# Regrouping VectorE's activation steps in the feed-forward phase of a pre-norm transformer layer: one group per tile instead of three lockstep stages over three tiles

## The reference

```python
x = x + attn(_layernorm(x), w_qkv, b_qkv, w_proj, b_proj)
# feed-forward, on _layernorm(x), w1: 1024 x 4096, w2: 4096 x 1024
h = float2fix(x @ w1 + b1, 8)             # round to multiples of 1/256
y = interp(h, 33 points of exact GELU on [-4, 4])
y = where(h > 4, h, where(h < -4, 0, y))
h = float2fix(y, 8)
out = float2fix(h @ w2 + b2, 8)
x = x + out
```

## Time and profile before

| what | us |
|---|---|
| median of 2 runs | 4179.5 (4175.3 and 4183.7) |
| the profiled execution | 4143.4 |
| its span on the slowest core (core 3), first to last instruction | 4141.9 |
| spans of the 8 cores | 4116.6 to 4141.9 |
| TensorE busy | 2703.5 (65%) |
| ScalarE busy | 2370.2 (57%) |
| VectorE busy | 2022.8 (49%) |
| GpSimd busy | 667.4 (16%) |

### The profile page before, as it was taken

One profiled execution on the slowest core, in us unless ns is written; L12 is line 12 of the kernel. 1 busy time (PEld: TensorE's weight loads), 2 busy tenths in 40 slices (PEclk: granted clock), 3 DMA queues, 4 the chain that ended last, 5 costly groups with the idle time before them and its releaser, 6 DMA issues.

```text
span 4141.9 us, 39884 instructions; the slowest of 8 cores (4116.6 to 4141.9 us)
## 1 busy us (share of the span) xinstructions
PE 2703.5 (65%) x10880; PEld 940.8 (23%) x10880; DVE 2022.8 (49%) x3166; ACT 2370.2 (57%) x2861; POOL 667.4 (16%) x1234
## 2 busy tenths in 40 slices
PE   0594757676769876768683455656665666667676
PEld 0241212111114311111111112222222222222222
DVE  2114434343430343434343466666767576666774
ACT  1223848484833484848481466666656566666662
POOL 1010000000001000000002233232323232332330
PEclk9997989898989998989896557877787777877788
DMA  5122010101022001010104533343434343443441
GB/s 105 51 31 92 29 54 28 48 4 43 4 63 33 10 4 43 4 43 4 43 4 102 92 56 55 63 64 63 68 67 71 54 79 52 68 65 65 59 77 44
DMA packets 204565, 207.43 MB, mean 50 GB/s; under 512 B 23744, under 2 KB 167104, under 8 KB 204352
## 3 DMA queue, kind: packets, MB, share of 16 engines
q0 software_dynamic: 169792, 95.82, 18.4%
q1 hardware_dynamic: 34560, 109.07, 8.0%
HBM read 257.52 MB, written 33.55 MB: 70 GB/s over the span
## 4 chain that ended last, share of the span: by engine, by line
PE 29%; DVE 18%; ACT 15%; DVEq 12%; ACTq 11%; issue 7%; DMA 7%; POOL 1%; SPq 0%; POOLq 0%
ACT PTb L625 12%; PE pAT L639 6%; PE pA L329 5%; DVEq L1035 5%; ACTq L995 5%; DMA xstream<-x 5%; PE pA L612 5%; ACTq L975 4%; PE pBT L641 3%; DVE ft L1016 3%; PE pA L1079 3%; PE pA L363 3%; DVEq L1018 3%; DVE ft L1025 2%; DVE fki L1010 2%
## 5 line engine op out<-in xcount | busy, mean ns | idle before, releaser
L625 ACT ACTIVATE PTb<-pA,negB 128x1024 bf16<-128x1024 f32 x1024 | 1106.3, 1113 | 473.8 <-PE pA L615 451.5
L937 PE MATMUL pA<-xn,w1s 128*128 128x512 bf16 x2048 | 672.1, 491 | 548.6 <-ACT ft L951 528.7
L798 POOL DMA_DIRECT2D w1s<-w x1024 | 556.7, 577 | 1221.3 <-PE pA L937 1196.9
L639 PE MATMUL pAT<-PTb,vtm 128*65 128x512 bf16 x1024 | 409.3, 400 | 271.0 <-ACT PTb L625 201.9
L1079 PE MATMUL pA<-w2b,gbuf 128*128 128x512 bf16 x2048 | 483.5, 397 | 77.4 <-DVEq L1018 45.0
L937 PEld LDWEIGHTS pA<-xn,w1s 128*128 128x128 bf16 x2048 | 225.6, 116 | 960.9 <-issue 841.9
L612 PE MATMUL pA<-qfm,kfm 64*128 64x512 bf16 x1024 | 404.5, 405 | 51.9 <-DVEq L713 50.6
L641 PE MATMUL pBT<-PTb,vtm 128*65 128x512 bf16 x1024 | 408.4, 399 | 0.0
L615 PE MATMUL pA<-qfm,kfm 64*128 64x512 bf16 x1024 | 404.7, 405 | 0.0
L963 ACT ACTIVATE fu<-ft,p 128x512 f32<-128x512 f32 x256 | 183.9, 718 | 298.6 <-DVEq L1035 298.6
L1010 DVE TENSOR_SCALAR fki<-ft 128x512 f32<-128x512 f32 x256 | 109.7, 429 | 471.4 <-ACT fji L978 450.4
(11 more groups left out here) (90 smaller groups left out, 3103.9 us busy)
## 6 DMA issues: line engine op xcount, KB each, us to landing
w1s<-w POOLq DMA_DIRECT2D x1024, 64.0 KB, 2.6
xstream<-x SPq DMA_DIRECT2D x80, 512.0 KB, 3.8
x1rd<-x1s SPq DMA_DIRECT2D x64, 512.0 KB, 5.7
x1s<-x1t SPq DMA_DIRECT2D x32, 512.0 KB, 2.9
out<-outt SPq DMA_DIRECT2D x64, 256.0 KB, 2.7
wstr<-wqkv POOLq DMA_DIRECT2D x96, 128.0 KB, 5.8
w2b<-w POOLq DMA_DIRECT2D x32, 256.0 KB, 25.5
attn<-stgB POOLq DMA_DIRECT2D x64, 64.0 KB, 1.9
```

What stands on the lines that cost most here:

```text
L625: sc.activation(PT[:, kt % 2, :], pA[:, off:off + 1024], AF.Exp, bias=negB[:, 0:1], scale=SCALE).then_inc(c_s.sem, 1)
L639: t.matmul(pAT[0:65, :], lhs[:, 2 * pr, :], PT[:, kt % 2, 0:512], start=(kt == 0), stop=(kt == NKT - 1), skip_group_check=True)
L798: gp.dma_start(out=w1s[:, sl, dc, :], in_=w1[dc * 128:(dc + 1) * 128, grp * 256:(grp + 1) * 256]).then_inc(c_lw[sl].sem, 16)
L937: ins = t.matmul(pA[:, hb * 512:(hb + 1) * 512], w1s[:, sl, dc, (hm % 2) * 128:(hm % 2 + 1) * 128], xn2[:, bi % 2, dc, :], start=(dc == 0) ...
```

## The change

VectorE's eight instructions per tile are no longer arranged in the stages P, Q and R over three tiles. Each of ScalarE's steps gets VectorE's work on the same tile right behind it: `act_E012(g)` holds the w1 product, S1 and VectorE's first two instructions (called Va below), `act_E34(g-1)` holds S2 and the next three (Vb), `act_E56(g-2)` holds S3 and the last three (Vc), `act_E78(g-3)` holds S4. Within Va, Vb and Vc every instruction needs the one before it and a drain stands between them; the last one carries the signal itself, with no drain behind it. The order of ScalarE's instructions stays. Core of the diff:

```diff
-        def act_S1(h):
+        def act_E012(h):
...
-            def ev(sc, hm=hm, hb=hb, i4=i4, w=w1_pe, vg=incQ.get(h - 2)):
+            def ev(sc, hm=hm, hb=hb, i4=i4, w=w1_pe, vg=e6_hist.get(h - 4)):
...
+            def ev(v, i=i, i4=i4, w=sid_done, sg=e5_hist.get(h - 3)):
+                v.wait_ge(c_s.sem, w)
+                if sg is not None:
+                    v.wait_ge(c_s.sem, sg)
+                v.tensor_scalar(fki[:, i4, :], ft[:, i4, :], -1152.5, 1152.5,
+                                ALU.max, ALU.min)
+                v.drain()
+                v.tensor_scalar(ft[:, i4, :], fki[:, i4, :], MC, -MC,
+                                ALU.add, ALU.add).then_inc(c_v.sem, 1)
...
-            def ev(sc, i=i, i4=i4, w=incQ[h]):
+            def ev(sc, i=i, i4=i4, w=e1_hist[(h, "va")]):
...
+            def ev(v, i=i, i4=i4, w=u5_done):
+                v.wait_ge(c_s.sem, w)
+                v.tensor_scalar(fki[:, i4, :], fu5[:, i, :], MC, -MC, ALU.add, ALU.add)
+                v.drain()
+                v.scalar_tensor_tensor(ft[:, i4, :], fki[:, i4, :], -1.0, fu5[:, i, :],
+                                       ALU.mult, ALU.add)
+                v.drain()
+                v.tensor_scalar(fu5[:, i, :], ft[:, i4, :], 0.5, None,
+                                ALU.add).then_inc(c_v.sem, 1)
...
-            def ev(sc, i4=i4, j=j, w=incP[h + 1]):
+            def ev(sc, i=i, j=j, w=e1_hist[(h, "vb")], fg=e6_hist.get(h - 2)):
                 sc.wait_ge(c_v.sem, w)
+                if fg is not None:
+                    sc.wait_ge(c_v.sem, fg)
...
+            def ev(v, i=i, i4=i4, j=j, w=s3_done):
+                v.wait_ge(c_s.sem, w)
+                v.tensor_sub(ft[:, i4, :], fji[:, j, :], fgl[:, j, :])
+                v.drain()
...
+                v.drain()
+                v.scalar_tensor_tensor(fu5[:, i, :], fgl[:, j, :], 256.0, fki[:, i4, :],
+                                       ALU.mult, ALU.add).then_inc(c_v.sem, 1)
...
-            def ev(sc, bi=bi, hm=hm, i=i, j=j, w=incR[h + 2],
+            def ev(sc, bi=bi, hm=hm, i=i, j=j, w=e6_hist[h],
...
-        w2mm_marks = (4, 7, 10, 13, 16, 19, 22, 25)
-        w2ev_marks = (6, 9, 12, 15, 18, 21, 24, 27)
+        w2mm_marks = (3, 6, 9, 12, 15, 18, 21, 24)
+        w2ev_marks = (5, 8, 11, 14, 17, 20, 23, 26)
...
-                act_S1(g)
+                act_E012(g)
...
-            if 0 <= g - 1 < NG:
-                act_S2(g - 1)
-            if 0 <= g - 2 < NG:
-                act_S3(g - 2)
-            if 0 <= g - 3 < NG:
-                act_S4(g - 3)
+            if g >= 1 and g - 1 < NG:
+                act_E34(g - 1)
+            if g >= 2 and g - 2 < NG:
+                act_E56(g - 2)
+            if g >= 3 and g - 3 < NG:
+                act_E78(g - 3)
...
-            if g <= NG + 1:
-                act_V(g, NG)
```

More of the change, by code:

```diff
@@ L914, in build @@
         e5_hist = {}
+        e6_hist = {}
         e8_hist = {}
[L916 to L919, removed]
-        def act_S1(h):
+        def act_E012(h):
             bi, hm = divmod(h, 32)
             hb = hm % 2
+            i = h % 3
             i4 = h % 4
@@ L955, in act_S1, with act_E34 @@
             e1_hist[h] = c_s.n
-        def act_S2(h):
+            sid_done = c_s.n
+            def ev(v, i=i, i4=i4, w=sid_done, sg=e5_hist.get(h - 3)):
[7 more added lines that the diff above has]
+                                ALU.add, ALU.add).then_inc(c_v.sem, 1)
+            p.on("vector", ev)
+            c_v.n += 1
+            e1_hist[(h, "va")] = c_v.n
+        def act_E34(h):
             i = h % 3
             i4 = h % 4
-            def ev(sc, i=i, i4=i4, w=incQ[h]):
+            def ev(sc, i=i, i4=i4, w=e1_hist[(h, "va")]):
                 sc.wait_ge(c_v.sem, w)
@@ L966, in act_S2, with act_E56 @@
             c_s.n += 1
-            u5_hist[h] = c_s.n
-        def act_S3(h):
+            u5_done = c_s.n
+            def ev(v, i=i, i4=i4, w=u5_done):
[7 more added lines that the diff above has]
+                                ALU.add).then_inc(c_v.sem, 1)
+            p.on("vector", ev)
+            c_v.n += 1
+            e1_hist[(h, "vb")] = c_v.n
+        def act_E56(h):
+            i = h % 3
             i4 = h % 4
             j = h % 2
-            def ev(sc, i4=i4, j=j, w=incP[h + 1]):
+            def ev(sc, i=i, j=j, w=e1_hist[(h, "vb")], fg=e6_hist.get(h - 2)):
                 sc.wait_ge(c_v.sem, w)
+                if fg is not None:
+                    sc.wait_ge(c_v.sem, fg)
                 sc.drain()
@@ L982, in act_S3, with act_E78 @@
             e5_hist[h] = c_s.n
-        def act_S4(h):
+            s3_done = c_s.n
+            def ev(v, i=i, i4=i4, j=j, w=s3_done):
+                v.wait_ge(c_s.sem, w)
+                v.tensor_sub(ft[:, i4, :], fji[:, j, :], fgl[:, j, :])
+                v.drain()
+                v.scalar_tensor_tensor(fki[:, i4, :], ft[:, i4, :], 256.0, fu5[:, i, :],
+                                       ALU.mult, ALU.mult)
+                v.drain()
+                v.scalar_tensor_tensor(fu5[:, i, :], fgl[:, j, :], 256.0, fki[:, i4, :],
+                                       ALU.mult, ALU.add).then_inc(c_v.sem, 1)
+            p.on("vector", ev)
+            c_v.n += 1
+            e6_hist[h] = c_v.n
+        def act_E78(h):
             bi, hm = divmod(h, 32)
@@ L1001, in act_S4 @@
             e8_hist[h] = c_s.n
[L1003 to L1052, removed]
@@ L1134, in build @@
             xn2_ready[0] = ln2_C2(0, tt)
-        w2mm_marks = (4, 7, 10, 13, 16, 19, 22, 25)
-        w2ev_marks = (6, 9, 12, 15, 18, 21, 24, 27)
+        w2mm_marks = (3, 6, 9, 12, 15, 18, 21, 24)
+        w2ev_marks = (5, 8, 11, 14, 17, 20, 23, 26)
         NG = NB * NHM
-        for g in range(NG + 6):
+        for g in range(NG + 3):
             if g < NG:
@@ L1154, in build @@
                     tt, st = divmod(hm - 3, 4)
-                    if st == 0 and tt < 4:
+                    if st == 0 and hm >= 3 and tt < 4:
                         ln2_L(bi + 1, tt)
```

## The result

| | before | changed |
|---|---|---|
| median, all executions | 4224.2 us (10) | 4090.3 us (11) |
| lowest execution | 4144.4 | 3965.7 |
| ratio, 95% interval | | 0.951 (0.945 to 0.958) |
| profiled execution | 4143.4 | 3963.7 |
| its span | 4141.9 | 3961.5 |

The change makes the kernel 4.9% faster. In many executions of either kernel the TensorE clock of one die is lower and the time some 3% longer, which is why the medians lie so far above the profiled executions; ratios and traces compare executions without that.

A forecast was written before the change was run, and what follows sets the result against it. A latency loop through P, Q, S2 and S3 (5.48 us) was taken to bound plain iterations. Gains of 224 and 6 less losses of 25 and 34 made 171 us, from the 4179.5 median to 4008 us; range 3950 to 4130.

The forecast's parts named there:

- The sum: Whole kernel: gains 224 and 6, losses 25 and 34, pipeline filling and emptying cancelling; 171 us saved.
- plain periods: Feed-forward iterations without extra work: 5.48 us becomes 4.6, saving 224 us over 255 periods.
- The loop P, Q, S2, S3 of 5.48 us: Plain iteration before: latencies 3.24 + 0.80 + 1.44 set the period while ScalarE and VectorE both idle.
- VectorE bounds at 4.6: Plain iteration after: Va 0.85, Vb 1.62, Vc 2.15 set the period; ScalarE's 4.05 fits under it.
- Starting a group costs nothing: Starts of Va, Vb, Vc with a wait: taken as 0 us; other end 0.99 us per iteration.
- Rival 1: Starting a group costs 0.19 us three times per iteration: 145 us lost, time 4153; chance 0.13.
- The layer norm tile: Iterations with layer norm: 9.8 and 7.3 us, 8.6 extra per tile against 8.8; 6 us gained over 28 tiles.
- Emptying a piece: VectorE emptying second-product pieces: 2.05 us each against 1.6 before; 25 us lost over 56 pieces.
- The first piece: Second product's first piece, one iteration earlier, delays S1(3): 8.4 us lost per block against 3.6; 34 us over seven blocks.
- Rivals 2 and 3: TensorE bounds through its low clock, time 4181, chance 0.04; VectorE holds up GpSimd's w1 load issues, time 4354, chance 0.04.

The follow-up runs named there:

- old_dup_gelu: Kernel before, half of S3's second Gelu (256 of 512 columns) done twice behind a drain; first to last S1 1877.8 us, before + 122.9.
- old_dup_add: Kernel before, the + 0.5 tensor_scalar in R done twice with a drain between; first to last S1 1804.7 us, before + 49.8.
- new_group_drains: Changed kernel with a drain that signals at the end of Va, Vb and Vc; first to last S1 1791.3 us, changed + 209.0.
- new_old_marks: Changed kernel with the second product's pieces at their former places, nothing else; first to last S1 1548.7 us, changed - 33.6.
- the interleaved version: Changed kernel, VectorE's eight instructions laid across tiles again, keeping per-step waits and signals on instructions, three drains; first to last S1 1486.8 us, changed - 95.5.
- mix_late_marks: The interleaved version with the second product's pieces one iteration later than their former places; first to last S1 1415.4 us, ratio to before 0.918.

## Why the prediction was right

The sum had 171 us; the profiled execution went from 4143.4 to 3963.7, and the phase it speaks of lost 172.6. The mechanism is the one that was forecast, and the terms hold one by one and not only in their sum. Read from the starts of VectorE's first instruction of every iteration (P before, Va now), against 5.48 before and 4.58 now: 229 us gained in plain periods (224 forecast), 7 at the layer norm tiles (6), 28 lost in emptying the pieces (25), 34 at the first pieces (34). By its steps:

- **The loop P, Q, S2, S3 of 5.48 us.** Shown by old_dup_gelu and old_dup_add.
- **VectorE bounds at 4.6.** Measured 4.58 to 4.62 with no idle time, Vc in 2668.68 - 2666.55 = 2.13 against 2.15. ScalarE's slack was put at 0.5 and is 0.5 to 0.7.
- **Starting a group costs nothing.** Right for the form that the change has: no bracket before L983 or L1015. Rival 1 was about a real cost, 0.18 to 0.26 us, but one that a signalling drain ahead brings with it; new_group_drains shows what it would have taken.
- **The layer norm tile.** 9.8 us forecast, 9.84 measured for the first iteration; 7.3 forecast and 7.18 measured for the second (2554.32 to 2561.50, where Vc ends). With the two iterations behind them, in which the copy of the transposes lies, a tile costs 8.4 to 8.7 extra on VectorE in block 0, where nothing else disturbs it; 8.6 was forecast. In S1 it looks otherwise: from hm = 9 of block 0 its periods are 11.7, 7.0, 4.0 and 4.0, because behind the stall ScalarE runs ahead at its own pace until it has to wait for VectorE again.
- **Emptying a piece.** Now it adds 1.87 in most iterations and 1.92 in the mean, where 2.05 was forecast; the waits are hidden under the instruction before. The 1.6 for the kernel before, which the prediction had only as what was left over, was too high as well. There a piece adds 1.0 in an iteration without layer norm work, because VectorE's 1.22 us of idle time take part of it (the L1010 ahead of the rows is the line below, 6.53 us before the next one), and about 2.0 beside layer norm work, 1.43 in the mean. The difference, 0.49 for each of 56, is 28 us against 25: two errors that cancel.

```profile
2902.11 0.43 DVE L1010 TENSOR_SCALAR fki<-ft 128x512 f32<-128x512 f32 x1 [0.34 <-ACT fji L978]
```

- **The first piece.** Va(3) came 14.1 us after Va(2) in block 1, not 13.0: its piece lasted 9.52 us and not 8.43. The piece of the earlier trace rows was the shortest of the seven before; their mean is 9.2, before and now (8.4 to 10.0). With it the cost per block was 4.5 before and 9.3 now, where 3.6 and 8.4 had been put: both 0.9 more, as the prediction said of a piece of another length, and the difference stays. It is 34 us, as new_old_marks measured (33.6).
- **Rivals 2 and 3.** S1 waited for TensorE in ten places, 100.8 us in all: three at the start and one at each block's first piece, none at later marks. GpSimd's issues of w1 loads kept their length:

```profile
L798 POOL DMA_DIRECT2D w1s<-w x1024: 528/566/931, 2252.0 to 3864.0; - x171
```

0.566 against 0.558 us in the median, with VectorE denser by a fifth in the plain iterations; that rival is out. The 3100 ns that the Trainium skill ("SBUF — State Buffer", the section named in the prediction) gives for a GpSimd-issued DMA beside a VectorE copy does not appear beside these instructions, none of which lasts longer than 0.7 us.

Off was the absolute time: 4008 forecast, 4090 measured as a median. The median of before rose as well, from 4179.5 (2 runs) to 4224.2 (10). The ratio forecast, 4008 / 4179.5 = 0.959, lies just outside the interval that was measured; set against the profiled execution it would be 3972 / 4143.4 = 0.959 and came out 0.957. The forecast had no step for what lifts the median, 82 us above 4008; that it stayed inside 3950 to 4130 for all that is luck, while the saving is not.

## What to carry to other kernels

When two engines that feed each other both idle in every period, look for the loop of latencies and take one link out of it; then add up the fuller engine's chain with its drains, because that sum, and not the sum of durations, was the new period here. Put the signal on the last instruction and not on a drain behind it, and fill drain gaps with independent instructions of neighbouring tiles: here these were worth 0.90 and 0.34 us per iteration. A burst on a third engine that must wait for the end of a stage belongs where its successor is not needed at once; moving it back by two iterations was worth 71 us in the interleaved version.

## What the runs showed of the hardware that was not expected

- A wait that is already met costs VectorE nothing behind an instruction that carries its own signal (L1020 to L960 in 0.60 us, the duration being 0.69), and there are 0.18 to 0.26 us of idle time at it behind a drain that signals. Without a wait the gap behind a signalling drain is 0.13 (L1016 to L1025 in the earlier trace rows), and behind a plain drain 0.08. The Trainium skill, "VectorE: DVE Perf Modes", section "The DRAIN you can't avoid", says that a semaphore after each operation costs nothing extra; these rows agree for signals on instructions. Of an explicit drain that signals it says nothing, and in new_group_drains that form did cost time.
- The half-width Gelu of 256 columns took 0.51 us where the full one of 512 took 0.71, and its drain another 0.07: halving the columns took away less than a third of the time.
- The first piece of the second product took 9.52 us behind 11.71 us of idle TensorE and 7.14 (mix_late_marks) behind a w1 product, for the same 32 matmuls. The granted clock over the piece was 0.74 in the one, 0.50 (1.2 GHz) in its first 4 us and 1.00 (2.4 GHz) in its last 3, and 0.99 in the other, whose w1 product had still run at 0.50.
